# Gated cross-attention and mixture-of-experts attention: the head reordered, two experts' gates spread by TensorE, the weights prepared in three turns

## What is computed

```python
x = x + tanh(g_xattn) * xattn(ctx_1024, layernorm(x), Wk, Wq, Wv)
# ffn part, on h = layernorm(x), n = all tokens:
logits = (h / |h|) @ (sim / |sim|) - sigmoid(gates)
w = softmax over the experts with logits > 0 (else the two largest)
q, k, v = [sum over e of w[n, e] * (h[n] @ proj[e]) for proj in (q_proj, k_proj, v_proj)]
o = softmax(q k^T / sqrt(128)) v          # inside each sequence
x = x + tanh(g_ffn) * sum over e of w[n, e] * (o[n] @ o_proj[e])
```

## Time and profile before

| | us |
|---|---|
| time, median of 3 runs (lowest, highest) | 800.66 (800.41, 801.44) |
| the profiled execution, its own time | 799.99 |
| its span, first to last instruction | 798.1 |
| TensorE busy in the span | 776.1 |
| VectorE busy | 607.2 |
| GpSimd busy | 483.0 |
| ScalarE busy | 433.8 |

### The profile page before, as it was taken

One profiled execution on the slowest core, in us unless ns is written; L12 is line 12 of the kernel. 1 busy time (PEld: TensorE's weight loads), 2 busy tenths in 40 slices (PEclk: granted clock), 3 DMA queues, 4 the chain that ended last, 5 costly groups with the idle time before them and its releaser, 6 DMA issues.

```text
span 798.1 us, 13995 instructions
## 1 busy us (share of the span) xinstructions
PE 776.1 (97%) x3999; PEld 418.1 (52%) x3999; DVE 607.2 (76%) x2037; ACT 433.8 (54%) x1129; POOL 483.0 (61%) x703
## 2 busy tenths in 40 slices
PE   7489999999999999999999999999999999999998
PEld 6445545555455555545555554555555455544444
DVE  2977787878787787778777787877878786775648
ACT  5554645556555655655565565456556555544445
POOL 3276657674746757474675747567574755765534
PEclk9789999999999999999999999999999999999999
DMA  6564476563655636365563636546364654543100
GB/s 192 136 216 159 162 219 174 169 209 94 209 161 164 189 106 204 97 210 167 151 191 106 202 109 209 166 150 186 101 207 116 208 160 139 163 135 116 53 14 28
DMA packets 97476, 122.57 MB, mean 154 GB/s; under 512 B 14611, under 2 KB 69111, under 8 KB 97399
## 3 DMA queue, kind: packets, MB, share of 16 engines
q1 hardware_dynamic: 96679, 121.59, 49.6%
q10 hardware_dynamic: 720, 0.08, 0.1%
HBM read 97.32 MB, written 24.31 MB: 152 GB/s over the span
## 4 chain that ended last, share of the span: by engine, by line
PE 88%; DVE 5%; DMA 2%; POOL 1%; ACT 1%; issue 1%; SPq 0%; DVEq 0%; ACTq 0%; POOLq 0%
PE acc_q L1380 20%; PE acc_k L1380 20%; PE acc_v L1380 20%; PE y L1409 9%; PE oT_p L1409 9%; PE m L1489 2%; PE m L1553 2%; DVE x_all L1175 1%; PE oT_p L1641 1%; PE m L1480 1%; PE m L1539 1%; DMA stage<-in_L_ffn_q_proj_dram 1%; PE m L1469 1%; POOL zq L658 1%; PE m L1529 1%
## 5 line engine op out<-in xcount | busy, mean ns | idle before, releaser
L658 POOL TENSOR_TENSOR zq<-zq_full,zq 128x512 f16<-128x512 f32 x256 | 297.8, 1170 | 222.4 <-ACT zq L743 222.2
L743 ACT ACTIVATE zq<-zq_full 128x512 f16<-128x512 f32 x256 | 160.1, 636 | 224.1 <-DVE zq_full L1145 224.0
L1175 DVE SCALAR_TENSOR_TENSOR x_all<-y,w_out,x_all 128x128 f32<-128x128 f32 x356 | 122.2, 343 | 96.1 <-issue 69.5
L1380 PE MATMUL acc_q<-zq,w_hi 128*128 128x512 f16 x510 | 193.3, 379 | 1.0 <-POOL zq L658 1.0
L1380 PE MATMUL acc_k<-zq,w_hi 128*128 128x512 f16 x510 | 193.2, 379 | 0.0
L1380 PE MATMUL acc_v<-zq,w_hi 128*128 128x512 f16 x510 | 193.2, 379 | 0.0
L1145 DVE TENSOR_TENSOR zq_full<-wq_bc,x2T_p 128x512 f32<-128x512 f32 x256 | 167.8, 668 | 2.5 <-DMA wq_bc<-w_rows 1.7
L1175 DVE SCALAR_TENSOR_TENSOR x_all<-oT_p,w_out,x_all 128x128 f32<-128x128 f32 x356 | 121.5, 341 | 0.0
L673 POOL TENSOR_TENSOR x_all<-stage,x_all 128x128 f32<-128x128 f32 x240 | 100.4, 456 | 19.8 <-DVE x_all L1175 13.3
L1380 PE MATMUL acc_q<-zq,w_lo 128*128 128x512 f16 x255 | 96.6, 379 | 0.0
L1380 PE MATMUL acc_v<-zq,w_lo 128*128 128x512 f16 x255 | 96.6, 379 | 0.0
(11 more groups left out here) (253 smaller groups left out, 1091.4 us busy)
## 6 DMA issues: line engine op xcount, KB each, us to landing
wq_bc<-w_rows SPq DMA_DIRECT2D x128, 512.0 KB, 4.5
blk_rows<-stage SPq DMA_DIRECT2D x26, 256.0 KB, 2.7
stage<-blk_rows SPq DMA_DIRECT2D x104, 64.0 KB, 2.0
blk_rows<-v_blk SPq DMA_DIRECT2D x15, 256.0 KB, 2.0
v_mix<-blk_rows SPq DMA_DIRECT2D x60, 64.0 KB, 2.9
blk_rows<-pc_blk SPq DMA_DIRECT2D x15, 256.0 KB, 4.1
pcT<-blk_rows SPq DMA_DIRECT2D x60, 64.0 KB, 2.0
out_dram<-x_all SPq DMA_DIRECT2D x15, 256.0 KB, 6.7
```

Source lines behind the costliest of these rows:

```text
L658: nc.gpsimd.tensor_tensor(zq[:, 1, e % Z_SLOTS, :], zq_full[:, e % F_SLOTS, :], zq[:, 0, e % Z_SLOTS, :], ALU.subtract).then_inc(zq_lo_poo ...
L743: nc.scalar.activation(zq[:, 0, e % Z_SLOTS, :], zq_full[:, e % F_SLOTS, :], ACT.Copy).then_inc(zq_hi_done, 1)
L1175: nc.vector.scalar_tensor_tensor(out=rows(x_all, g, b0 + b), in0=bank[:, tok(j)], scalar=w_out[:, g % 2, e, b0 + b:b0 + b + 1], in1=rows(x ...
L1380: last = nc.tensor.matmul(acc[m][:], w[:, m, s, :], zq[:, half, s % Z_SLOTS, :], start=(s == 0 and n == 0), stop=(s == E - 1 and n == 2))
```

## The change

SyncE no longer waits for Wq and Wk before it goes on, issues q's weights ahead of the contexts, and group 1's x ahead of v's weights. VectorE's head takes stats(1) and x2_norm_inverse(0) ahead of V's maximum, the logits ahead of the scales, and `x_max(1)` ahead of gate_softmax(0). The gates of experts 0 and 1 of group 0 no longer go through DRAM: `gate_diagonal(e)` multiplies the identity by the gates into wq_bc, `gate_spread(e)` multiplies it by ones on TensorE, which leaves the spread gate in PSUM, and zq_scale takes it from there. `spread_q` starts with the pair of experts 2 and 3. weight_high and weight_low of q, k and v are made in three parts, experts 0 to 3, 4 to 9 and 10 to 15; the first two in the head, the third in iteration 0 (ScalarE at step 6, VectorE at step 8). ScalarE takes x2_norm(1), which stood at step 1, ahead of zq_high(0, 3). keep_busy(8) in the head becomes keep_busy(6) and a keep_busy(4) ahead of px_transpose(1).

```diff
+BY_PE = 2
+PARTS = ((0, 4), (4, 10), (10, 16))
...
             def head():
-
-                sp.wait_ge(kq_in, 16 * 2)
+                load_weights(Q, q_proj)
                 sp.dma_start(zq_full[0:S, 0:PRE].rearrange("p k (b c) -> p (k b) c", b=G),
                              c_v[:, G:G * (PRE + 1), :]).then_inc(ctx_pre_in, 16)
-                load_weights(Q, q_proj)
                 load_weights(K, k_proj)
+                load_x(1)
                 load_weights(V, v_proj)
-                load_x(1)
                 load_weights(O, o_proj)
                 load_x(2)
                 weight_rows(0)
-                for j in range(W_SLOTS):
+                for j in range(BY_PE // 2, W_SLOTS):
                     spread_q(0, j)
...
-            def weight_high(m):
+            def weight_high(m, part=0):
                 act.wait_ge(scales_done, 1 if m < O else 2)
-                nc.scalar.activation(w_hi[:, m], stage[:, m], ACT.Copy,
+                nc.scalar.activation(split_part(w_hi, m, part), split_part(stage, m, part), ACT.Copy,
                                      scale=w_up[:, m:m + 1]).then_inc(hi_done[m], 1)
...
+            def gate_diagonal(e):
+                wait(dve, w_ready, 1)
+                nc.vector.tensor_tensor(wq_bc[:, 0, e].rearrange("p (b t) -> p b t", b=G),
+                                        ident[:].unsqueeze(1).broadcast_to([P, G, P]),
+                                        w_new[:, 0, e].unsqueeze(2).broadcast_to([P, G, P]),
+                                        ALU.mult).then_inc(w_diag_done, 1)
...
+            def gate_spread(e):
+                pe.wait_ge(w_diag_done, e + 1)
+                pe.wait_ge(logit_read, 1)
+                nc.tensor.matmul(SPREAD_BANKS[e][:], ones[:], wq_bc[:, 0, e], start=True,
+                                 stop=True).then_inc(w_spread_ps, 1)
...
+                    if i == 0 and s == 6:
+                        for m in (Q, K, V):
+                            weight_high(m, 2)
...
+                    if i == 0 and s == 8:
+                        for m in (Q, K, V):
+                            weight_low(m, 2)
...
+                    for part, (first, _) in enumerate(PARTS):
+                        if (i, s) == (0, first):
+                            pe.wait_ge(hi_done[m], part + 1)
+                            pe.wait_ge(lo_done[m], part + 1)
...
-                for g in range(1, PRE + 1):
-                    ctx_transpose(g)
-                px_transpose(0)
-                kx_product(1)
-                att_product(0)
-                vx_product(1)
+                ctx_transpose(1)
+                px_transpose(0)
+                for g in range(2, PRE + 1):
+                    ctx_transpose(g)
+                att_product(0)
+                for g in range(1, PRE + 1):
...
                 px_transpose(1)
+                gate_spread(0)
+                gate_spread(1)
                 att_product(1)
```

More of the change, by code:

```diff
@@ L411, in vx_bank, with split_part @@
             return (acc[V], oT_p, acc[K])[g - 1] if 1 <= g <= PRE else m0
+        SPREAD_BANKS = (m0, oT_p)
+        def split_part(t, m, part):
+            experts = slice(*PARTS[part]) if m < O else slice(0, E)
+            return t[:, m, experts].rearrange("p e h -> p (e h)")
         def ctx_slot(g):
@@ L889, in head @@
                 vx_out(0)
-                ctxT_out(1)
                 pxT_out(0)
[L892 to L896, removed]
+                for g in range(1, PRE + 1):
+                    ctxT_out(g)
+                for g in range(1, PRE):
                     kxT_out(g)
@@ L899, in head @@
                 x2_norm(0)
+                kxT_out(PRE)
                 x2T_out(0)
-                weight_high(Q)
+                vx_out(PRE)
+                x2T_move(0)
                 x_norm(1)
@@ L904, in head @@
                 xnT_out(1)
-                x2T_move(0)
-                weight_high(K)
                 x_exps(1)
                 pxT_out(1)
-                weight_high(V)
-                for e in range(LEAD):
-                    zq_high(0, e)
+                for m in (Q, K, V):
+                    weight_high(m)
+                zq_high(0, 0)
+                weight_high(Q, 1)
+                weight_high(K, 1)
+                zq_high(0, 1)
+                weight_high(V, 1)
+                zq_high(0, 2)
+                x2_norm(1)
+                zq_high(0, 3)
             def body(i):
@@ L1136, in zq_scale @@
             def zq_scale(g, e):
-                if e == 0:
-                    wait(dve, x2T_moved, g + 1)
                 if g == 0 and e < PRE:
                     wait(dve, ctxT_ps, e + 2)
+                if g == 0 and e < BY_PE:
+                    wait(dve, x2T_sb, 1)
+                    wait(dve, w_spread_ps, e + 1)
+                    nc.vector.tensor_tensor(zq_full[:, e, :], SPREAD_BANKS[e][:], x2T[:],
+                                            ALU.mult).then_inc(zq_full_done, 1)
+                    return
+                if e == (BY_PE if g == 0 else 0):
+                    wait(dve, x2T_moved, g + 1)
                 if e % 2 == 0:
                     j = e // 2
-                    wait(dve, wq_in[j % W_SLOTS], 16 * (PAIRS // W_SLOTS * g + j // W_SLOTS + 1))
+                    n = PAIRS // W_SLOTS * g + j // W_SLOTS + (1 if j % W_SLOTS else 0)
+                    wait(dve, wq_in[j % W_SLOTS], 16 * n)
                 wait_zq_low(dve, *before(g, e, F_SLOTS))
@@ L1237, in head @@
                 weight_max(K)
+                first_stats(1)
                 setup_gate()
+                x2_norm_inverse(0)
                 weight_max(V)
+                gate_logits(0)
                 share_largest(0)
-                first_stats(1)
+                gate_mask(0)
+                x_max(1)
+                gate_softmax(0)
+                gate_diagonal(0)
                 weight_scales(0)
[L1243 to L1249, removed]
+                gate_diagonal(1)
                 x_sum(1)
                 zq_scale(0, 0)
+                for m in (Q, K, V):
+                    weight_low(m)
                 zq_scale(0, 1)
-                weight_low(V)
+                x1_add(1)
                 zq_scale(0, 2)
-                x1_add(1)
                 second_stats(1)
+                weight_low(Q, 1)
+                weight_low(K, 1)
                 zq_scale(0, 3)
+                weight_low(V, 1)
                 first_stats(2)
```

26 lines of the change are left out of this document (15 added, 11 removed).

## The result

| | before | after |
|---|---|---|
| time, median (lowest, highest), us | 800.66 (799.98, 801.44) | 804.08 (803.59, 806.34) |
| its span in the profiled execution | 798.1 | 801.8 |

The ratio is 1.0047, its 95% interval 1.0033 to 1.0061: the change makes the kernel slower, by 3.4 us between the medians and 3.7 between the spans. The forecast was 802.1, within 798.6 to 803.9; the median lies 0.2 above that range.

The account below looks back on a forecast made before the run. TensorE was taken as busy 97% of the span, so only time before 92 us could move. -1.4 + 2.9 = +1.5 on 799.99 gave 801.5, and 0.67 for the median 802.1, within 798.6 to 803.9.

Parts of the forecast that it names:

- Early loads: Start of the head: q's weights and contexts issued sooner delay the small loads by 0, with 0.5 kept for the range.
- The 1.66: Head, first attention: x1_add(0) starts at 17.36 instead of 19.02, 1.66 us sooner.
- The term of -1.4: Head up to expert 4 of group 0: it starts at 53.0 instead of 54.43, 1.4 us sooner.
- Clock at the spreads: TensorE's two gate spreads: high clock level back by 33 us, 0.9 to 1.15 each; at the low level twice 0.86.
- rival 2: Clock still low at both spreads and the attention product, which ends later than 38.0: -0.1 + 3.0, 803.6; chance 0.25.
- The scores at the low level: Group 0's score products in the head: 2.0 us at the lower clock level, as before.
- rival 3: Clock doesn't fall before the scores, 1.1 instead of 2.0: 0.9 less, 801.2; chance 0.12.
- Exclusion between VectorE and GpSimd: Head and iteration 0: weight_low pieces and GpSimd's steps take turns, each holding the other for an instruction; short steps wait too.
- Rival 1: Weight_low pieces short enough that GpSimd and VectorE pass each other: -3.5 + 1.75, 798.9; chance 0.20.
- Part three: Iteration 0: third weight_low pieces take 3.85 on VectorE, TensorE stands ahead of group 2's px transpose: +2.9.
- The 1.7 at expert 10: Iteration 0: TensorE waits 1.7 ahead of expert 10 for group 2's weights, as part of the 2.9.
- Rival 4: Iteration 0: new VectorE work doesn't meet group 2's exponentials, VectorE running further ahead; second term about 0, 799.2; chance 0.06.

Follow-up runs that it names:

- e1_loads_back: The changed kernel with SyncE's wait for Wq and Wk and the contexts ahead of q's weights again, as before: 803.02 us, ratio 1.0034.
- r6_fill: e1_loads_back with keep_busy(18), filler products on TensorE, ahead of expert 3: 801.87 us, ratio 1.0029.
- r5: The changed kernel with first_stats(2) and zq_scale(0, 3) ahead of the three second pieces of weight_low: 803.58 us, ratio 1.0039.
- e5: The changed kernel with the weights in two parts, experts 0 to 3 and 4 to 15, and no third turn: 805.51 us, ratio 1.0060.
- r11: r10 with the third weight pieces of q and k at step 4: 801.67 us, ratio 1.0015, one execution of 1357.8 left out.
- r12: r10 with all of O's preparation later, from step 12 of iteration 0 to step 3 of iteration 1: 804.51 us, ratio 1.0053.
- r15: r10 with O's maximum at step 10, shares at 11 and 12, rounding at 13, low part at step 2 of iteration 1: 801.85 us, 1.0019.
- r17: r15 with O's share products at steps 12 and 13 and 6 idle products each ahead of experts 2 and 3: 800.47 us, ratio 0.9996.
- r10: Changed kernel, loads back, first_stats(2) and zq_scale(0, 3) before weight_low, x2_norm(1) behind zq_high(0, 3), x2T_out(1) before x_norm(2): 800.76 us, 1.0006.

## Why the prediction was wrong, point by point

**Early loads: the step that failed.** I wrote "I take 0 and keep 0.5 for the range". Measured, the gates' load was used at 8.69, 1.7 later than with the loads back (6.98), TensorE stood 1.24 for Wk until 9.03, x_norm(0) came at 9.73 (8.24 in e1_loads_back), px's transposes at 17.22 instead of 14.9, and x1_add(0) 2.56 later than forecast. With the loads back q's weights set it again, and it starts at 18.61 to 19.44 over ten traces, on both sides of the 19.02 before the change. The 1.66 were to be had only if the early loads held up nothing. The 2.56 run through: w_blk is ready at 35.62 against my 32.8, 2.8 late, and expert 4 starts at 56.25 against 53.0, 3.25 late. The term of -1.4 measured +1.8. The rest of the chain can be tested apart from the loads: with them back and the clock held (r6_fill) expert 4 starts at 53.79, 2.5 ahead of the changed kernel and 0.8 behind my 53.0.

**Clock at the spreads.** "I take the high level back by 33 us" failed too: it came back at 38, the spreads took 1.7 and 1.0, and the attention product ended at 40.24, behind the 38.0 at which rival 2 was to decide. With it zq_full(2) is 3.25 behind its forecast (43.75 for 40.5) where w_blk is 2.8: some 0.5 came in between. Beside e1_loads_back, where the clock was back at 36 and the spreads took 1.02 and 1.13, it is 1.0: from w_blk to zq_full(2) 8.13 against 7.11. That holds both the clock and three weight_low pieces of 512, which took 2.97 here and 2.07 there; no run parts them. So rival 2's condition held and its time, 803.6, is the nearest, but it is near by luck: most of the loss is the loads', which no rival named.

**The scores at the low level** took 1.99 (I said 2.0), so rival 3 is out.

**Exclusion between VectorE and GpSimd.** It is there: three pieces took 3.80 (I said 3.85), GpSimd's steps 0.82 and 0.87, r5 shows 0.23 with the neighbour gone, e5 1.62 beside pieces twice as long. The Trainium skill (SBUF — State Buffer, "Who interferes with whom") says that whoever issues first holds the port for the whole instruction, and all three agree. From zq_full(2) to the end of second_rstd(1) it is 5.89, forecast 5.9, though by luck, two errors that cancel: zq_low(0,2) ended 2.56 behind zq_full(2) instead of 1.85 (I left out zq_high's turn), and GpSimd's steps took 3.33 from there instead of 4.05. Rival 1 is out.

**Part three.** The mechanism was right, the size not: +2.9 forecast, +1.8 measured, 1.9 by e5. VectorE reached zq_full(12) 11.43 behind expert 4, before it was 12.55; its logit step took 0.22 at 61.10, where it had taken 1.23. I had carried VectorE's place over from the trace of before as if it were fixed to expert 4. The 1.7 at expert 10 was 0.32. ScalarE's three pieces took 2.58 and were hidden, as forecast. Rival 4 is out, though it had the direction of this error.

**Sum.** Forecast -1.4 + 2.9 = +1.5; measured +1.82 + 1.81 = +3.63. The first term was off by 3.2 and the second by 1.1 the other way, so the total looks better than its parts. Two slips of 0.1 in the working change nothing: 31.15 + 0.5 + 1.28 is 32.9 and not 32.8, and 73.40 + 3.85 is 77.25 and not 77.15.

## What to carry to other kernels

A large load issued while small ones are under way was not free here: look at the first users of the small loads, and ask which of them starts the first chain. Where TensorE waits several microseconds, as ahead of expert 3 in e1_loads_back, look at the granted clock behind the wait and count it too. Where an engine's row has no gap, moving a piece within the row moves the stall (r11). Work taken out of the row took the stall at px away (r12, r15, r17), but each time a wait came where the work went; look first whether every engine that it touches has a gap there.

## What was not expected of the hardware

Moving a weight load of 1 MB (issued at 2.80) and one of contexts of 462 KB (at 3.68) ahead delayed loads issued before them, on their own queue (Wk, issued at 2.16 and used at 9.03 after a wait of 1.24) and on ScalarE's (gates_b, issued at 1.76 and used at 8.69 for 6.98 with the loads back; sim, 9.47 for 7.59). A TensorE wait of 4.6 us cost another 1.5 in clock. And executions of one kernel spread wider in the versions with such waits: r15 had 799.80 to 804.16, against 799.93 to 801.37 of the kernel before beside it. The time goes with the mean granted clock of the execution: in r6_fill the five at 0.994 and above took 801.15 to 801.87, the three at 0.989 and below 803.51 to 804.65; in r15 the three at 0.994 and above took 799.80 to 801.62, the other eight 801.27 to 804.16. Elsewhere it does so less (r10's lowest, 799.48, was at 0.991). Where in an execution the clock is lost is known only for the one that was profiled, so what lets it fall in some and not in others stays open, as does what a version below the kernel before would need.
